# Two layers of convolutional self-attention in float32 on one core: loops written out, and the prologue's statistics, staging and second projection in a new order

## The chip, the cores and the metric

The kernel runs on 1 core of one Trainium2 chip. The metric is the device time in microseconds, median of several runs. Of one more run there is a profile with every instruction of every engine; its span is the time from the first to the last instruction, and times in the trace count from the span's start.

## The reference, cut to what matters

Both layers compute, for each of 8 images of 256 channels and 32 x 32 = 1024 positions:

```python
xn  = group_norm(x, 32 groups) * gamma + beta
qkv = w_qkv @ xn + b_qkv                 # 8 heads of 32 channels
m   = softmax((q / 32**.25).T @ (k / 32**.25))     # 1024 x 1024 for each head
out = x + w_proj @ (m @ v) + b_proj
```

The second layer takes the first one's output, has weights of its own and no bias on q, k and v. Everything is float32.

## The kernel before

There are 16 blocks (layer and image), and each is worked through in two slots of 4 heads, so 32 slots, numbered 0 to 31. In a slot 64 units follow each other (2 halves of 512 queries x 8 tiles of 128 keys x 4 heads). For each unit TensorE multiplies a tile of transposed scores (`scores_t`, L396), ScalarE takes the exponential (`exp`, L631), and TensorE later multiplies it with the values (`weighted_values`, L442). The softmax needs the maximum of each query's row before. So another score tile per unit, in the other orientation, runs 40 units ahead (`AHEAD`): `scores_for_max` (L421) on TensorE, `max_unit` (L708) on VectorE, three PSUM banks in turn, so that TensorE is at most three units ahead of VectorE. After each eight of them VectorE reduces once more (L716), and SP copies that head's row of negative maxima into row 96 of the queries by four small transfers (`load_row`, L300); row 96 of the keys holds ones, so that `scores_t` subtracts the maximum. `scores_t` waits for its row at the first tile of each head and half.

q and k are kept as a float32r part and the rest. `project_qk` (L464) on TensorE makes a half of q or k in four matmul instructions, `qk_high` (L650) on ScalarE writes the high part, `qk_low` (L725) on VectorE the low one, both into staging tiles. From there SP copies for each head three pieces of q and three of k, 32 partitions of 4 KB each (`stage_head`, L290), so that one matmul over 96 partitions has all three products. `project_v` (L472) and `v_out` (L733) make the values. All this is done for the next slot or block in between the units, at fixed places (`DENSE_AT` and others), and so are group statistics: `channel_stats` (L741) and `add_quarters` (L746) on VectorE, `mean_square` and `scale_and_shift` on GpSimd, `group_stats` (L487) on TensorE, `group_stats_out` (L656) and `normalise` (L663) on ScalarE. GpSimd sums the exponentials (L876).

Each engine's program is written by hand and runs in its own order; semaphores tie them together. TensorE's program is written out in full (`write_slots`). ScalarE, VectorE and GpSimd use `run_slots`: slot 0 plain, then a loop of 7 passes over 4 slots (slots 1 to 28), then slots 29 to 31 plain. In the loop the semaphore values to wait for are computed in registers. SP's program has slots 0 to 4 plain, a loop of 2 passes (slots 5 to 12), slots 13 to 16 plain, a loop of 3 passes (slots 17 to 28), and the rest plain.

Before slot 0 there is a prologue. Image 0 is loaded, then weights, then image 1. Image 0's statistics (VectorE, GpSimd, TensorE, ScalarE) lead to its normalising; TensorE projects q and k of the first four heads into four banks, then the values; ScalarE and VectorE empty the banks. SP waits until all low parts are written (`qkl_done` 4) and issues the 24 staging copies. VectorE, behind its value evacuations, does image 1's statistics; TensorE multiplies them (`group_stats(1, ps_v)`), and then 40 leading units of `scores_for_max` follow (w = 0 to 39). Between them TensorE projects q and k of the other four heads: part r after unit w = 8r, its low part on VectorE after unit w = 8r + 2. ScalarE's first `qk_high` of these overwrites the staging tiles, so it waits until all 24 copies are done.

Of the kernel before, what the change touches and what calls it, by code (L numbers as in the profile page):

```python
# [25 lines left out]
F32 = mybir.dt.float32  # L26
# [8 lines left out]
HD = C // HEADS  # L35
SCALE = float(HD) ** -0.5
P = 128
CT = C // P
HG = HEADS // CT
NT = S // P  # L40
HALF = 512
NH = S // HALF
# [21 lines left out]
ROWS_AT = 7  # L64
STATS_AT = (23, 26, 28, 33)
# [17 lines left out]
def plain(n):  # L83
    return Slot(n, n // 2, n % 4)


def looped(i, k):
    return Slot(LOOP_SLOTS * i + LOOP_FROM + k, 2 * i + (LOOP_FROM + k) // 2, (LOOP_FROM + k) % 4)
# [6 lines left out]


def run_slots(eng, slot):

    slot(plain(0), first=True)
    with eng.Fori(0, LOOPS) as i:  # L100
        for k in range(LOOP_SLOTS):
            slot(looped(i, k))
    for n in range(LOOP_FROM + LOOPS * LOOP_SLOTS, SLOTS):
        slot(plain(n), has_next=n + 1 < SLOTS, has_second=n + 2 < SLOTS, has_third=n + 3 < SLOTS)
# [54 lines left out]
def attention_layers(nc, x, w_qkv, w_proj, pars, bias_v, bias_proj, ident_in, group_in, out):  # L159
    nc.disable_value_cache = True  # L160
    ctx = ExitStack()
    with ctx:
# [96 lines left out]
        def _(sp):  # L259
# [57 lines left out]
            sp.dma_start(wp[:, :, :], w_proj[0]).then_inc(wproj_loaded, 16)  # L317
            for h in range(HG):
                stage_head(0, 0, h)
# [46 lines left out]
            with sp.Fori(1, turn) as i:  # L366
                body(i, 0, 0)
            body(turn, 1, 0)
            with sp.Fori(turn + 1, LOOPS) as i:
                body(i, 1, 1)  # L370
# [9 lines left out]
        def _(pe):  # L380
# [103 lines left out]
            def group_stats(j, bank):  # L484

                pe.wait_ge(mv_summed, j + 1)
                mm = pe.matmul(bank[:, 0:2 * CT], group[:, :], channel_mv[:, :, :], start=True, stop=True)  # L487
                mm.then_inc(gm_ready, 1)
# [86 lines left out]
            for r in range(4):  # L575
                for kt in range(CT):
                    project_qk(0, 0, r, kt, start_banks[r])
            for r in range(4):

                pe.wait_ge(qkl_done, r + 1)  # L580
                for t in range(2):
                    project_v(0, r, t, start_banks[r])
            pe.wait_ge(gm_done, 1)
            group_stats(1, ps_v)

            pe.wait_ge(v_done, 4)
            pe.wait_ge(ones_row_set, 2)

            for w in range(AHEAD):
                scores_for_max(-1, 1, w - AHEAD + UNITS)  # L590
                if w % MAX_GROUP == 0 and w // MAX_GROUP < 4:
                    r = w // MAX_GROUP
                    if r:

                        pe.wait_ge(qkl_done, 4 + r)
                    for kt in range(CT):
                        project_qk(1, 0, r, kt)
            write_slots(slot)
# [15 lines left out]
        def _(act):  # L614
# [74 lines left out]
            for part in range(CT * NH):  # L689
                normalise(1, 1, part)  # L690
# [3 lines left out]
            run_slots(act, slot)  # L694
# [4 lines left out]
        def _(dve):  # L699
# [109 lines left out]
            add_quarters(0)  # L809
            for r in range(4):  # L810
                qk_low(0, 0, 0, r, start_banks[r])
# [4 lines left out]
            for part in range(CT * NH):  # L816
                channel_stats(1, 1, part)
            add_quarters(1)
            for w in range(AHEAD):
                max_unit(-1, w - AHEAD + UNITS)  # L820
                if w % MAX_GROUP == 2 and w // MAX_GROUP < 4:
                    qk_low(1, 1, 0, w // MAX_GROUP)
            run_slots(dve, slot)
# [6 lines left out]
        def _(pool):  # L830
# [62 lines left out]
            scale_and_shift(0, 0)  # L893
            for b in range(2):
                pool.memset(ks[b][MROW:MROW + 1, :, :].bitcast(F32), 1.0).then_inc(ones_row_set, 1)

                pool.wait_ge(ones_row_set, b + 1)
            mean_square(1)
            scale_and_shift(1, 1)
            run_slots(pool, slot)  # L900


# [46 lines left out]
```

## Time and profile before

| | us |
|---|---|
| median of 3 runs | 2149.19 (2148.03 to 2149.98) |
| profiled execution | 2149.15 |
| its span | 2147.4 |
| TensorE busy | 2092.4 (97%) |
| GpSimd busy | 1791.0 (83%) |
| VectorE busy | 1696.5 (79%) |
| ScalarE busy | 1238.8 (58%) |

Busy time is the sum of an engine's instructions. A busy share near 100% in a stretch means that the engine sets the pace there; where it is lower, the rows say what the engine waited for. TensorE's clock has two levels; the granted clock is 1.00 where it had the full one and 0.50 where it had half. A row of the windows below has: start and end of the stretch, its length, then busy time (and number of instructions) of TensorE's matmuls, its weight loads, VectorE, ScalarE and GpSimd, then the granted clock, the DMA engines' mean busy share and GB/s. A row of a timeline has: start, length, engine, line, what it writes and reads, how many in a row, and in brackets the idle time before it with what ended it.

### The profile page before, as it was taken

To read this page: it belongs to the slowest core of one execution; us is meant where nothing else is said; L and a number is where in the kernel's file an instruction comes from. 1 tells how busy PE (TensorE), PEld (TensorE's weight loads), DVE (VectorE), ACT (ScalarE), POOL (GpSimd) and SP (SyncE) were. 2 spreads that over 40 slices of the span, in tenths; PEclk is the share of its full clock that TensorE was granted. 3 is DMA by queue.
4 is the path that set the end of the run, shared out by engine and by line. 5 is a ranking of instruction groups with operands and counts; after the bars stand their busy time and mean duration, and the time that the engine had idled before them with its cause. 6 is when DMAs were issued, how large, how long until landed. Compare 5 with 4: busy or idle time off the path is not lost.

```text
span 2147.4 us, 37263 instructions
## 1 busy us (share of the span) xinstructions
PE 2092.4 (97%) x10552; PEld 1160.0 (54%) x10552; DVE 1696.5 (79%) x2896; ACT 1238.8 (58%) x2321; POOL 1791.0 (83%) x567
## 2 busy tenths in 40 slices
PE   5999999999999999999999999999999999999998
PEld 3455555555555555555555555555555555556542
DVE  3878888788887888887887888878887788888881
ACT  2355656566565665656565565655656556565654
POOL 2398988888887988978988888978889889889895
PEclk8799999999999999999999999999999999999999
DMA  4333243322334233244322434223343222433211
GB/s 125 60 57 63 61 100 80 92 44 59 84 80 100 62 68 65 65 100 99 85 50 52 98 79 99 55 56 70 80 99 75 70 56 60 99 80 80 54 27 40
DMA packets 208741, 157.04 MB, mean 73 GB/s; under 512 B 166528, under 2 KB 166784, under 8 KB 208512
## 3 DMA queue, kind: packets, MB, share of 16 engines
q1 hardware_dynamic: 208512, 154.48, 32.0%
q8 instruction: 84, 1.38, 0.3%
q14 instruction: 145, 1.19, 0.2%
HBM read 36.39 MB, written 16.78 MB: 25 GB/s over the span
## 4 chain that ended last, share of the span: by engine, by line
PE 90%; POOL 4%; issue 2%; DVE 2%; SPq 1%; ACT 1%; DMA 1%; DVEq 0%; ACTq 0%; POOLq 0%
PE ps_t L396 23%; PE ps_m L421 21%; PE ps_v L442 21%; PE ps_d L464 10%; PE ps_m L456 6%; PE ps_d L479 5%; PE ps_d L472 5%; POOL acc L876 3%; DVE raw_max L708 1%; SPq L290 1%; ACT pt L631 0%; DMA qs<-neg_max 0%; PE ps_m L464 0%; DMA par<-pars_dram 0%; PE ps_t L487 0%
## 5 line engine op out<-in xcount | busy, mean ns | idle before, releaser
L631 ACT ACTIVATE pt<-ps_t 128x512 f32<-128x512 f32 x2048 | 1110.2, 599 | 835.2 <-PE ps_t L396 823.5
L708 DVE TENSOR_REDUCE raw_max<-ps_m 128x1 f32<-128x512 f32 x2048 | 1316.8, 685 | 304.7 <-PE ps_m L421 265.2
L876 POOL TENSOR_TENSOR acc<-acc,pt 128x2048 f32<-128x2048 f32 x317 | 1450.7, 4576 | 32.7 <-POOL gn_c L861 5.5
L421 PE MATMUL ps_m<-ks,qs 96*128 96x512 f32 x2048 | 994.1, 487 | 14.4 <-DVE raw_max L708 13.2
L396 PE MATMUL ps_t<-qs,ks 97*128 97x512 f32 x2048 | 842.9, 413 | 13.1 <-ACT pt L631 11.7
L396 PEld LDWEIGHTS ps_t<-qs,ks 97*128 97x128 f32 x2048 | 389.7, 190 | 379.3 <-ACT pt L631 158.6
L876 POOL TENSOR_TENSOR acc<-pt 128x2048 f32<-128x2048 f32 x64 | 292.7, 4573 | 264.8 <-ACT pt L631 264.8
L421 PEld LDWEIGHTS ps_m<-ks,qs 96*128 96x128 f32 x2048 | 391.8, 191 | 193.2 <-DVE raw_max L708 115.0
L442 PE MATMUL ps_v<-pt,v 128*32 128x512 f32 x4096 | 492.7, 597 | 0.0
L464 PE MATMUL ps_d<-xn,wq 128*128 128x512 f32 x500 | 263.6, 611 | 5.8 <-ACT xn L663 5.8
L442 PEld LDWEIGHTS ps_v<-pt,v 128*32 128x32 f32 x4096 | 119.5, 109 | 250.4 <-issue 171.0
L479 PE MATMUL ps_d<-att,wp 128*128 128x512 f32 x256 | 130.8, 593 | 3.8 <-DVE att L764 2.9
L472 PE MATMUL ps_d<-wq,xn 128*128 128x256 f32 x488 | 125.1, 378 | 0.0
L464 PEld LDWEIGHTS ps_d<-xn,wq 128*128 128x128 f32 x500 | 98.1, 197 | 31.5 <-issue 11.0
L472 PEld LDWEIGHTS ps_d<-wq,xn 128*128 128x128 f32 x488 | 92.3, 189 | 17.5 <-issue 0.5
L753 DVE STREAM_TRANSPOSE turned<-ps_m 128x512 f32<-128x512 f32 x64 | 45.9, 717 | 40.4 <-PE ps_m L456 38.8
L716 DVE TENSOR_REDUCE neg_max<-raw_max 128x4 fp32r<-128x8 f32 x256 | 41.4, 162 | 41.3 <-DVE raw_max L708 40.2
L456 PE MATMUL ps_m<-pt,ones 128*32 128x512 f32 x536 | 71.6, 607 | 0.3 <-DVE raw_max L708 0.2
L456 PE MATMUL ps_m<-acc,ones 128*32 128x512 f32 x512 | 68.6, 595 | 0.0
L725 DVE SCALAR_TENSOR_TENSOR stage_ql<-ps_d,par,stage_qh 128x512 fp32r<-128x512 f32 x63 | 47.3, 751 | 21.0 <-ACT stage_qh L650 15.0
L479 PEld LDWEIGHTS ps_d<-att,wp 128*128 128x128 f32 x256 | 48.6, 191 | 17.5 <-issue 5.2
L775 DVE SCALAR_TENSOR_TENSOR res<-ps_d,bp,res 128x512 f32<-128x512 f32 x64 | 47.5, 743 | 12.2 <-PE ps_d L479 12.2
(49 smaller groups left out, 540.2 us busy)
## 6 DMA issues: line engine op xcount, KB each, us to landing
ks<-stage_kh SPq DMA_DIRECT2D x256, 128.0 KB, 2.4
qs<-stage_qh SPq DMA_DIRECT2D x256, 128.0 KB, 2.4
ks<-stage_kl SPq DMA_DIRECT2D x128, 128.0 KB, 2.4
qs<-stage_ql SPq DMA_DIRECT2D x128, 128.0 KB, 2.5
qs<-neg_max SPq DMA_DIRECT2D x1024, 0.5 KB, 2.0
xn<-x_dram SPq DMA_DIRECT2D x16, 512.0 KB, 4.5
res<-x_dram SPq DMA_DIRECT2D x16, 512.0 KB, 4.5
between<-res SPq DMA_DIRECT2D x32, 256.0 KB, 2.3
```

The source lines that it names most:

```text
L396: pe.matmul(ps_t[score_bank(s.g, u)][:, :], ks[s.qk][0:KROWS + 1, h, t * P:(t + 1) * P], qs[s.qk][0:KROWS + 1, h, hf * HALF:(hf + 1) * HAL ...
L421: pe.matmul(ps_m[max_bank(u)][:, :], qs[b][0:KROWS, h, c:c + P], ks[b][0:KROWS, h, kf * HALF:(kf + 1) * HALF], start=True, stop=True).then ...
L442: mm = pe.matmul(ps_v[HD * h:HD * (h + 1), :], v[s.v][:, t, c:c + HD], pt[t % 4][:, h, :], start=(t == 0), stop=(t == NT - 1))
L456: mm = pe.matmul(ps_m[bank][HD * h:HD * (h + 1), :], ones[:, :], tile[:, h, :], start=(k == 0), stop=(k == len(tiles) - 1))
L464: mm = pe.matmul(bank[:, :], wq[:, kt, c:c + P], xn[parity][:, kt, hf * HALF:(hf + 1) * HALF], start=(kt == 0), stop=(kt == CT - 1))
L472: mm = pe.matmul(bank[:, t * C:(t + 1) * C], xn[parity][:, kt, (2 * r + t) * P:(2 * r + t + 1) * P], wq[:, kt, 2 * C:3 * C], start=(kt == ...
L479: mm = pe.matmul(ps_d[:, :], wp[:, kt, ct * P:(ct + 1) * P], att[:, kt, hf * HALF:(hf + 1) * HALF], start=(kt == 0), stop=(kt == CT - 1))
L631: act.activation(pt[t % 4][:, h, :], ps_t[score_bank(s.g, u)][:, :], ACT.Exp, scale=SCALE).then_inc(exp_done, 1)
L708: dve.tensor_reduce(raw_max[:, e % 2, t, kf:kf + 1], ps_m[max_bank(u)][:, :], AX.X, ALU.max)\
L725: dve.scalar_tensor_tensor(out=lo[:, cols], in0=bank[:, :], scalar=par[:, parity, 4 + 2 * which + g:5 + 2 * which + g], in1=hi[:, cols].bi ...
L775: dve.scalar_tensor_tensor(out=r, in0=ps_d[:, :], scalar=bp[:, ct:ct + 1], in1=r, op0=ALU.add, op1=ALU.add).then_inc(proj_done, 1)
L876: pool.tensor_tensor(acc[hf][:, :, :], a[:, :, :], pt[t % 4][:, :, :], ALU.add).then_inc(pool_added, 1)
```

## The change

- `run_slots` and the loops of SP's program are gone. All engines use `write_slots`, and SP's `for` runs in Python, so that every slot's instructions stand in the program with constant semaphore values.
- In the prologue VectorE does image 1's statistics right behind image 0's. TensorE's `group_stats(1, ps_v)` stands ahead of the value projection. GpSimd's `mean_square(1)` and `scale_and_shift(1, 1)` stand ahead of the memsets of the ones rows, and TensorE waits for these only ahead of slot 0.
- The 24 staging copies of the prologue are issued by two engines: the 12 into the queries by SP, the 12 into the keys by ScalarE behind `group_stats_out(1, ps_v)`.
- The second projection's part r stands after unit w = 8r + 6 (before: 8r), its low part after unit w = 8r + 10 (before: 8r + 2). ScalarE normalises a quarter of image 1 after each of its four `qk_high` (before: all four ahead of them).

```diff
+START_QK, START_LOW = 6, 2
...
-def run_slots(eng, slot):
-
-    slot(plain(0), first=True)
-    with eng.Fori(0, LOOPS) as i:
-        for k in range(LOOP_SLOTS):
-            slot(looped(i, k))
-    for n in range(LOOP_FROM + LOOPS * LOOP_SLOTS, SLOTS):
-        slot(plain(n), has_next=n + 1 < SLOTS, has_second=n + 2 < SLOTS, has_third=n + 3 < SLOTS)
...
@@ SP @@
-            for h in range(HG):
-                stage_head(0, 0, h)
+            sp.wait_ge(qkl_done, NH)
+            for h in range(HG):
+                for r, part in enumerate(("qh", "qh", "ql")):
+                    sp.dma_start(qs[0][HD * r:HD * (r + 1), h, :].bitcast(F32),
+                                 stage[part][HD * h:HD * (h + 1), :].bitcast(F32)).then_inc(staged[h], 16)
...
-            with sp.Fori(1, turn) as i:
+            for i in range(1, turn):
                 body(i, 0, 0)
             body(turn, 1, 0)
-            with sp.Fori(turn + 1, LOOPS) as i:
+            for i in range(turn + 1, LOOPS):
                 body(i, 1, 1)
@@ TensorE @@
+            pe.wait_ge(gm_done, 1)
+            group_stats(1, ps_v)
             for r in range(4):
 
                 pe.wait_ge(qkl_done, r + 1)
                 for t in range(2):
                     project_v(0, r, t, start_banks[r])
-            pe.wait_ge(gm_done, 1)
-            group_stats(1, ps_v)
 
             pe.wait_ge(v_done, 4)
-            pe.wait_ge(ones_row_set, 2)
-
             for w in range(AHEAD):
                 scores_for_max(-1, 1, w - AHEAD + UNITS)
-                if w % MAX_GROUP == 0 and w // MAX_GROUP < 4:
+                if w % MAX_GROUP == START_QK and w // MAX_GROUP < 4:
...
+
+            pe.wait_ge(ones_row_set, 2)
@@ ScalarE @@
-            for part in range(CT * NH):
-                normalise(1, 1, part)
+
+            act.wait_ge(qkl_done, 4)
+            for h in range(HG):
+                for r, part in enumerate(("kh", "kl", "kh")):
+                    act.dma_start(ks[0][HD * r:HD * (r + 1), h, :].bitcast(F32),
+                                  stage[part][HD * h:HD * (h + 1), :].bitcast(F32)).then_inc(staged[h], 16)
 
             for r in range(4):
                 qk_high(1, 1, 0, r)
-            run_slots(act, slot)
+                normalise(1, 1, r)
+            write_slots(slot)
@@ VectorE @@
             add_quarters(0)
+            for part in range(CT * NH):
+                channel_stats(1, 1, part)
+            add_quarters(1)
...
-            for part in range(CT * NH):
-                channel_stats(1, 1, part)
-            add_quarters(1)
             for w in range(AHEAD):
                 max_unit(-1, w - AHEAD + UNITS)
-                if w % MAX_GROUP == 2 and w // MAX_GROUP < 4:
-                    qk_low(1, 1, 0, w // MAX_GROUP)
-            run_slots(dve, slot)
+                if w % MAX_GROUP == START_LOW and w >= MAX_GROUP:
+                    qk_low(1, 1, 0, w // MAX_GROUP - 1)
+            write_slots(slot)
@@ GpSimd @@
             scale_and_shift(0, 0)
+            mean_square(1)
+            scale_and_shift(1, 1)
             for b in range(2):
                 pool.memset(ks[b][MROW:MROW + 1, :, :].bitcast(F32), 1.0).then_inc(ones_row_set, 1)
 
                 pool.wait_ge(ones_row_set, b + 1)
-            mean_square(1)
-            scale_and_shift(1, 1)
-            run_slots(pool, slot)
+            write_slots(slot)
```

## Rows read from the trace of the kernel before

**Rows 1.** The page: busy time, share of the span, instructions.

```profile
PE 2092.4 (97%) x10552; PEld 1160.0 (54%) x10552; DVE 1696.5 (79%) x2896; ACT 1238.8 (58%) x2321; POOL 1791.0 (83%) x567
```

**Rows 2.** Windows of slots 1, 3, 5, 25, 28 and 29.

```profile
136.53:201.68 65.15, 64.72 (x340) 37.59 (x338) 54.14 (x94) 37.48 (x72) 55.51 (x24) 1.00 0.43 82
...
265.49:330.07 64.58, 64.50 (x340) 37.69 (x338) 54.12 (x94) 37.36 (x72) 54.68 (x23) 1.00 0.36 83
...
393.76:461.22 67.46, 65.02 (x339) 37.67 (x338) 54.02 (x94) 37.35 (x72) 54.62 (x23) 1.00 0.34 80
...
1690.95:1758.15 67.20, 65.03 (x339) 37.67 (x338) 54.02 (x94) 37.36 (x72) 54.58 (x23) 1.00 0.34 80
...
1886.56:1950.25 63.69, 63.69 (x321) 34.51 (x320) 52.03 (x89) 39.93 (x75) 57.67 (x14) 1.00 0.31 68
1950.25:2013.92 63.67, 63.67 (x338) 37.31 (x336) 51.85 (x89) 37.69 (x71) 54.70 (x13) 1.00 0.31 67
```

**Rows 3.** Timeline around slot 5's start: start, length, what, [idle before, releaser].

```profile
396.58 1.57 ACT L631 ACTIVATE pt<-ps_t 128x512 f32<-128x512 f32 x3 [2.26 <-PE ps_t L396]
...
398.32 1.89 DVE L708 TENSOR_REDUCE raw_max<-ps_m 128x1 f32<-128x512 f32 x3 [3.20 <-issue]
...
399.06 0.50 PE L421 MATMUL ps_m<-ks,qs 96*128 96x512 f32 x1 [1.33 <-DVE raw_max L708]
```

**Rows 4.** Table of waits, whole run: total, times, longest.

```profile
DVE raw_max L708 <- issue: 18.2, 6, 3.2
```

**Rows 5.** Timeline of slot 1, and its wait in the whole run's table.

```profile
171.49 0.47 PE L396 MATMUL ps_t<-qs,ks 97*128 97x512 f32 x1 [0.36 <-DMA qs<-neg_max]
...
PE ps_t L396 <- DMA qs<-neg_max: 0.4, 1, 0.4
```

**Rows 6.** The prologue: timeline of SP's first and last staging copy, then windows.

```profile
27.71 0.64 SPq L290 DMA_DIRECT2D ks<-stage_kh  x1
...
42.35 0.60 SPq L290 DMA_DIRECT2D qs<-stage_ql  x1
...
12.00:13.00 1.00, 0.00 (x0) 0.00 (x0) 0.00 (x0) 0.00 (x0) 0.77 (x4) 1.00 0.03 10
...
29.00:44.00 15.00, 10.21 (x31) 6.40 (x30) 6.60 (x11) 3.10 (x5) 2.59 (x11) 0.77 0.91 206
...
45.80:52.60 6.80, 5.25 (x8) 2.41 (x8) 4.50 (x8) 0.11 (x1) 0.00 (x0) 0.50 0.03 0
80.00:90.00 10.00, 9.92 (x43) 5.94 (x42) 8.13 (x16) 6.63 (x13) 4.54 (x1) 0.83 0.41 79
```

**Rows 7.** Timeline of the prologue from the last value evacuation on.

```profile
33.11 0.69 DVE L733 TENSOR_TENSOR v<-ps_m,bv 128x512 f32<-128x512 f32 x1 [1.03 <-PE ps_m L472]
33.72 2.46 DVE L741 BATCH_NORM_STATS2 stats<-xn 128x6 f32<-128x512 f32 x4
37.46 0.56 PE L487 MATMUL ps_v<-channel_mv,group 128*128 128x4 f32 x2 [4.39 <-DVE channel_mv L746]
37.88 0.77 PE L421 MATMUL ps_m<-ks,qs 96*128 96x512 f32 x1
38.69 0.69 DVE L708 TENSOR_REDUCE raw_max<-ps_m 128x1 f32<-128x512 f32 x1 [1.38 <-PE ps_m L421]
45.22 0.69 ACT L650 ACTIVATE stage_qh<-ps_d,par 128x512 fp32r<-128x512 f32 x1 [1.59 <-DMA qs<-stage_ql]
45.94 0.75 DVE L725 SCALAR_TENSOR_TENSOR stage_ql<-ps_d,par,stage_qh 128x512 fp32r<-128x512 f32 x1 [2.12 <-ACT stage_qh L650]
46.61 3.07 DVE L708 TENSOR_REDUCE raw_max<-ps_m 128x1 f32<-128x512 f32 x5
49.20 3.60 PE L464 MATMUL ps_d<-xn,wq 128*128 128x512 f32 x4
53.06 1.29 DVE L708 TENSOR_REDUCE raw_max<-ps_m 128x1 f32<-128x512 f32 x2 [2.58 <-PE ps_m L421]
79.00 0.63 PE L396 MATMUL ps_t<-qs,ks 97*128 97x512 f32 x1
```

## The prediction

> **What bounds the kernel now.** I read the page's busy line first: TensorE is busy 97% of the span, 2092.4 of 2147.4 us, no other engine over 83% [rows 1]. So time can be won only where TensorE stands idle, some 55 us. The windows then place it: I cut the trace at the first transposed-score matmul (L396) of each of the 32 slots. A slot of odd number with statistics takes 64.58, 64.56, 64.57 us (slots 3, 7, 27) and TensorE is busy for all but 0.1 us of it. Slots 5, 9, 13, 17, 21 and 25 take 67.20 to 67.46 us with 2.2 to 2.4 us idle [rows 2]. They are the first slot of a repeated pass of the loops. The zoom on slot 5 says why: ScalarE's first exponential comes 2.26 us late though its matmul is done, VectorE then idles 3.20 us with "issue" as its only cause, and TensorE waits 1.33 us for VectorE alone [rows 3]. The table of waits has this "issue" wait exactly six times, 18.2 us in all [rows 4]. Slot 1, where the loops are entered without a jump back, has none of it, and slot 29, straight code on every engine after the loops, none either [rows 2]. The jump back is what costs.
>
> The rest is at the start: the first L396 runs at 79.00 us [rows 7]. The chain there is: projections; 24 staging transfers issued one by one by SP, 27.71 to 42.95 us, 0.635 us each [rows 6]; ScalarE's first evacuation of the second projection, which waits for the last of them until 45.22; VectorE's low part, 45.94 to 46.69, before which only three of the 40 leading maxima are done; then 37 maxima and three more projections up to slot 0 [rows 7].
>
> **The change, part by part.** *Loops written out.* It removes six jumps back. Six slots sum to 403.75 us (67.46, three of 67.27, 67.28, 67.20); at slot 3's length they are 6 x 64.57 = 387.4, a gain of 16.3. The nearest other row is slot 1: 65.15 us, 0.57 longer than slot 3. It lost this at 171.49, where TensorE waited 0.36 us for SP's row of negative maxima to land [rows 5]. The late jumps covered that: a TensorE that comes 2.7 us later finds its rows there. If all six slots hit it, the gain is 6 x 2.13 = 12.8. The table of waits has such a wait once in the whole run [rows 5], so I charge one hit, 0.6, and take 15.7. The register instructions of the loops go too. Slot 29 without them and without group statistics takes 63.67, even slot 28 with them 63.69 [rows 2]: they are hidden behind TensorE, and I take 0. The end of the range: where a slot's statistics make TensorE wait for ScalarE, 14 times, each may lose about one 0.1 us step, 1.4 us of gain in all.
>
> SP's own straight code issues the same transfers in the same order; only its late arrival behind the jump goes. For the fetching of more code I take 0; the cover is that it runs ahead, as for TensorE's program, and its failing is a rival below.
>
> *Statistics of image 1 earlier.* VectorE's four (2.46 us at 33.72) and the quarter sum move into its idle time before 20.75. Their image is there: the DMA share is down to 0.03 in 12 to 13 us [rows 6]. They end near 15, and nothing waits. TensorE's group matmul moves ahead of the V projection and pushes that back by its 0.42 us (37.46 to the next matmul at 37.88). The last V evacuation, 33.11 to 33.80, ends at 34.2, and the leading scores start at 34.3 instead of 37.88 [rows 7]. Head 0 must be staged by then: its last transfer was issued at 30.92 and two queues don't make it later. GpSimd's memsets of the ones rows (7.07 us) go behind its scaling, to end at about 37, long before their new wait at the first slot. Normalising image 1, 2.93 us of ScalarE, is spread between evacuations; the first slot wants it 22 units in. Both cost 0.
>
> *Staging on two queues.* SP issues the q copies, ScalarE the k copies. Issue alone would shrink from 15.2 us to 12 x 0.635 = 7.6, and the last copy would land at 37.4. But in 29 to 44 us the 16 DMA engines are busy 0.91 already, at 206 GB/s [rows 6]. So 16 us of landing (29 to 45) can shrink to 0.91 x 16 = 14.6: 1.4 us earlier, 43.6. Issue of a DMA by ScalarE isn't in this trace; nearest is SP's 0.60 us, so 7.6 us there, ending at 35.3, or later if the full engines hold it back. Queued behind it is only the evacuation that waits for all 24 copies anyway. Bounds for the term: 0 to 1.4.
> The Trainium skill, "DMA: Bandwidth & Descriptors", section "Issuing engines are not separate DMA queues", says the same against this edit: transfers from several queues run on the same 16 engines, and only issue time is saved. By issue time alone the last landing would be 7.6 us earlier, by the rule with this trace's 0.91 1.4 us.
>
> *Second projection later among the leading scores.* It moves from the 1st, 9th, 17th and 25th unit to the 7th, 15th, 23rd and 31st, the low parts from the 3rd to the 11th and on. So VectorE isn't stopped after three maxima. From 34.3 (first maximum about 0.7 later, as 38.69 follows 37.88) it does 11 maxima at 0.614 us (5 in 3.07 [rows 7]), 6.8, and one stall on a projection, 2.6, and is through at 44.4. ScalarE's high part is ready at 43.6 + 0.2 + 0.7 = 44.5. The low part thus ends at 45.3, 1.4 before 46.69, with eight more maxima and a 0.1 us row maximum behind it, 5.0. What follows is as before, three projections, each of which makes VectorE idle (2.58 us at 53.06, the first of three alike, up to 2.8 [rows 7]). Gain 1.4 + 5.0 = 6.4 us. Bounds: 5.0 if the copies land no sooner; about 8 if the first projection stalls VectorE little and the copies come early. The wait for the ones rows, now ahead of the first slot, is long met. The first slot begins at half clock as before: 0.83 granted in 80 to 90 us [rows 6] is a third of ten at half, some 1.7 us lost. It may be none or twice that.
>
> **Sum.** 15.7 + 6.4 = 22.1 us. The profiled execution took 2149.15 us, span 2147.4 and 1.8 around it, which is the median of the runs (2149.19). 2149.15 - 22.1 = 2127.0 us, span about 2125.3.
>
> **Rivals.** *The projection's clock.* In 45.8 to 52.6 TensorE had 0.50, the 1.2 GHz level, after a stretch with less to do, and its four matmuls took 3.60 us [rows 6, 7]. Three earlier projections at 2.4 GHz would take 1.8, and the three stalls of 2.6 would nearly go: 6 us more, 2121.0. Against it: in all three groups the full level came behind the projection and was gone before the next. 8%.
> *The start gains nothing.* Copies on two queues get in each other's way, or the rows of the leading units come late, and the first slot starts at 79 as before: 2149.15 - 16.3 = 2132.9. Against: the DMA engines are idle from 45 on, and VectorE is visibly stopped. 8%.
> *The stall isn't the jump's.* A jump costs next to nothing, and something else in those six slots makes the engines late; it would stay, and only the start's 6.4 us come: 2142.8. Against it: slots 1 and 29 issue the same work and have no such wait [rows 2, 4]. 4%.
> The Trainium skill, "Advanced Engine Details and Errata", section "Control Flow Timing", would have it so: about 108 ns for a compare-and-branch, 0.65 us for six. The trace disagrees, with 3.20 us on VectorE after one jump.
> *Straight code starves.* If ScalarE or VectorE ran out of instructions at each new block of code as they do at the jump, each would cost TensorE some 2.7 us (67.27 - 64.57). From 8 such stalls the gain is gone; one in each of the 28 slots that were looped gives 76 - 22 = 54 us more, 2203. Against: TensorE runs 2 x 10552 instructions [rows 1] straight, and slots 0 and 29 to 31 are straight on all engines; VectorE's only "issue" waits are the six at the jumps [rows 2, 4]. 4%.
>
> **From cases to numbers.** Forecast 2127.0 with 73%, its own range 2123.5 (22.1 + 0.6 for no late row + 1.4 for the statistics + 1.6 for the start at 8) to 2131.5 (12.8 + 5.0 = 17.8). The clock rival adds the low end, 2120.5, the start rival the high end, 2133; left out are the last two and 3% unnamed. About 0.2% (4.3 us) is what a measurement of this kernel can tell from no change. Faster by more: the first three cases, the fourth (6.4 us) and most of the rest, 0.94. Within: 0.02. Slower: 0.04.
>
> **What would show it.** Slots 5, 9, ... 25 at 64.6 us (65.2 where a row is late) and no six "issue" waits: the loops right. The first L396 at 72 to 74 us; SP and ScalarE both issuing from 27.7; ScalarE's first second-projection evacuation near 43.8, not 37.4; the leading scores from 34.3; three stalls of 2.5 us left. Slots of 63.7 and 64.6 elsewhere unchanged. The forecast is wrong if "issue" waits appear in straight code, if rows land late in most odd slots, or if the copies land well after 45.

## The result, and the profile after

| | before | after |
|---|---|---|
| median, us | 2149.15 (2148.03 to 2149.98, 4 runs) | 2118.19 (2112.97 to 2119.25, 4 runs) |
| profiled execution, us | 2149.15 | 2112.97 |
| its span, us | 2147.4 | 2111.2 |
| mean granted clock in it | 0.990 | 0.996 |
| first slot starts at, us | 79.0 | 63.6 |
| slots 1 to 28, us | 1813.7 | 1791.1 |

The ratio is 0.9851 (95% interval 0.9834 to 0.9868): 31 us faster. Forecast were 22.1, 2127.0 us, with a range down to 2120.5. The direction and most mechanisms were right, the size was not. The profiled execution is the fastest of the four by 5 us; why is told in experiment 1. Two executions further down fell in a slow state and count in no ratio: one of experiment 1 (2956.3 us, clock 0.655) and one of the kernel with one queue (2159.8 us, clock 0.944).

From the page of after: TensorE's busy line, then queues (packets, MB, share). In before the last queue, which fetches instructions, had 145 packets and 1.19 MB; q10 is ScalarE's new queue.

```profile
PE 2073.6 (98%) x10552; PEld 1148.2 (54%) x10552; DVE 1698.3 (80%) x2896; ACT 1248.4 (59%) x2321; POOL 1790.4 (85%) x567
...
q10 hardware_dynamic: 576, 1.57, 0.3%
...
q14 instruction: 72, 0.59, 0.1%
```

Windows of after for slots 1, 3, 5, 28 and 29, then for slots 1 to 28 as one:

```profile
120.80:185.15 64.35, 64.21 (x340) 37.45 (x339) 54.14 (x94) 37.86 (x72) 55.94 (x24) 1.00 0.38 83
248.72:313.06 64.34, 64.20 (x339) 37.45 (x338) 54.12 (x94) 37.85 (x72) 55.33 (x23) 1.00 0.42 83
376.64:440.98 64.34, 64.20 (x340) 37.46 (x338) 54.13 (x94) 37.86 (x72) 55.34 (x23) 1.00 0.36 83
...
1848.28:1911.85 63.57, 63.57 (x321) 34.33 (x320) 52.10 (x89) 40.14 (x75) 56.94 (x14) 1.00 0.31 67
1911.85:1975.52 63.67, 63.67 (x337) 37.32 (x336) 51.87 (x89) 37.73 (x71) 54.91 (x13) 1.00 0.31 67
...
120.80:1911.85 1791.05, 1789.11 (x9213) 1004.96 (x9212) 1487.30 (x2535) 1092.03 (x2031) 1572.72 (x492) 1.00 0.34 76
```

Against [rows 2]: slot 5 lost its late start (67.46 to 64.34), but slot 3, which never had one, is shorter too (64.58 to 64.34), and so is slot 28 (63.69 to 63.57). Slot 29, straight code in both, kept its 63.67 to the hundredth.

The start of after, as a timeline, with ScalarE's issues as ACTq:

```profile
23.13 1.26 SPq L313 DMA_DIRECT2D qs<-stage_qh  x2
...
26.57 0.60 ACTq L688 DMA_DIRECT2D ks<-stage_kh  x1
...
33.48 4.28 DVE L708 TENSOR_REDUCE raw_max<-ps_m 128x1 f32<-128x512 f32 x7 [0.59 <-PE ps_m L416]
...
36.36 1.88 PE L459 MATMUL ps_d<-xn,wq 128*128 128x512 f32 x4
...
38.51 0.69 DVE L708 TENSOR_REDUCE raw_max<-ps_m 128x1 f32<-128x512 f32 x1 [0.75 <-PE ps_m L416]
...
39.65 0.69 ACT L645 ACTIVATE stage_qh<-ps_d,par 128x512 fp32r<-128x512 f32 x1 [13.84 <-DMA ks<-stage_kh]
...
41.10 0.74 DVE L725 SCALAR_TENSOR_TENSOR stage_ql<-ps_d,par,stage_qh 128x512 fp32r<-128x512 f32 x1
...
63.56 0.40 PE L391 MATMUL ps_t<-qs,ks 97*128 97x512 f32 x1
```

Against [rows 6, 7]: SP's first copy goes out at 23.1 instead of 27.7, the last has landed by 39.6 instead of 45.2, eleven maxima are done before the first low part instead of three, and a projection takes 1.88 us instead of 3.60 and stops VectorE for 0.75 to 0.89 us instead of 2.6. The windows say what the DMA engines and the clock did (share 1.02, clock 1.00):

```profile
26.50:38.00 11.50, 10.10 (x39) 6.73 (x37) 7.08 (x12) 0.00 (x0) 8.44 (x7) 1.00 1.02 227
...
45.80:52.60 6.80, 4.72 (x13) 2.26 (x13) 5.87 (x12) 1.47 (x3) 0.00 (x0) 1.00 0.05 3
```

Part of this isn't the edit's. The clock became full at 19.8 us here and at 21.9 in before, in the middle of the first projection, whose instructions are the same in both. Its fourth low part ends at 26.54 us instead of 27.68, so everything behind it starts 1.1 us sooner. Over the kernels with the changed order that follow, this low part ends anywhere from 26.3 to 27.8 us (25.4 where the first projection is given a warm clock), whatever the edit behind it. Comparisons of first slots below have to be read with that in mind.

In the profiles the 36.2 us of span are 15.4 before the first slot, 0.3 in slot 0, 22.7 in slots 1 to 28, less 2.2 after them (a stretch at half clock at 2102 fell on the last projection: 3.46 us for four matmuls, 1.96 before).

### The profile page after: what moved, and what is told of

It reads as the page before. It is cut to its first block, busy times and chain, and to the rows that moved or that the text cites. A ratio compares the mean times of both kernels' runs of the same rounds, so it can differ in the third digit from the quotient of the medians.

```text
span 2111.2 us, 31126 instructions
## 1 busy us (share of the span) xinstructions
PE 2073.6 (98%) x10552; PEld 1148.2 (54%) x10552; DVE 1698.3 (80%) x2896; ACT 1248.4 (59%) x2321; POOL 1790.4 (85%) x567
## 4 chain that ended last, share of the span: by engine, by line
PE 93%; POOL 4%; DVE 1%; ACT 1%; issue 0%; DMA 0%; SPq 0%; ACTq 0%; POOLq 0%; DVEq 0%
PE ps_t L391 24%; PE ps_m L416 21%; PE ps_v L437 21%; PE ps_d L459 10%; PE ps_m L451 6%; PE ps_d L474 5%; PE ps_d L467 5%; POOL acc L876 3%; DVE raw_max L708 1%; ACT pt L626 1%; PE ps_m L467 0%; PE ps_m L459 0%; PE ps_t L482 0%; DMA par<-pars_dram 0%; ACT xn L658 0%
## 5 line engine op out<-in xcount | busy, mean ns | idle before, releaser
L626 ACT ACTIVATE pt<-ps_t 128x512 f32<-128x512 f32 x2048 | 1121.9, 599 | 799.0 <-PE ps_t L391 783.5
L708 DVE TENSOR_REDUCE raw_max<-ps_m 128x1 f32<-128x512 f32 x2048 | 1336.6, 686 | 294.4 <-PE ps_m L416 292.2
L459 PE MATMUL ps_d<-xn,wq 128*128 128x512 f32 x500 | 256.8, 596 | 5.7 <-ACT xn L658 5.7
L451 PE MATMUL ps_m<-pt,ones 128*32 128x512 f32 x536 | 71.6, 609 | 0.2 <-DVE raw_max L708 0.2
L775 DVE SCALAR_TENSOR_TENSOR res<-ps_d,bp,res 128x512 f32<-128x512 f32 x64 | 47.5, 743 | 14.2 <-PE ps_d L474 14.2
L645 ACT ACTIVATE stage_qh<-ps_d,par 128x512 fp32r<-128x512 f32 x63 | 43.0, 683 | 21.5 <-DMA ks<-stage_kh 13.8
```

What stands on the lines that cost most here:

```text
L451: mm = pe.matmul(ps_m[bank][HD * h:HD * (h + 1), :], ones[:, :], tile[:, h, :], start=(k == 0), stop=(k == len(tiles) - 1))
L459: mm = pe.matmul(bank[:, :], wq[:, kt, c:c + P], xn[parity][:, kt, hf * HALF:(hf + 1) * HALF], start=(kt == 0), stop=(kt == CT - 1))
L626: act.activation(pt[t % 4][:, h, :], ps_t[score_bank(s.g, u)][:, :], ACT.Exp, scale=SCALE).then_inc(exp_done, 1)
L708: dve.tensor_reduce(raw_max[:, e % 2, t, kf:kf + 1], ps_m[max_bank(u)][:, :], AX.X, ALU.max)\
L775: dve.scalar_tensor_tensor(out=r, in0=ps_d[:, :], scalar=bp[:, ct:ct + 1], in1=r, op0=ALU.add, op1=ALU.add).then_inc(proj_done, 1)
```

## The experiments

**1. Is the start always like this?** The changed kernel unaltered.

> The changed kernel unaltered, to see whether its start always goes as in the profile. Theory A (clock): the granted clock of the prologue differs from execution to execution. Then spans fall with the granted share: about 2111 us at 0.996, about 2116.5 at 0.992 to 0.993, and if this profile has the lower share its first transposed score starts near 68 to 69 us instead of 63.6, with projections that take 3.4 to 3.6 us instead of 1.9; slots 1 to 28 take 1791 us in both. Theory B: the 5 us lie elsewhere (slots or the end); then a slower profile still starts its first slot near 63.6 and slots 1 to 28 take about 1796.

Measured: ratio 0.9855 (0.9829 to 0.9882). Theory A in kind; the first slot is later than its 68 to 69 us. Spans of the two sets of runs go by the granted share: 2111.2 to 2111.7 us at 0.996, 2112.0 at 0.995, 2116.2 to 2116.6 at 0.993, 2117.2 to 2119.9 at 0.992, 2120.3 at 0.991. This profile has 0.992; its timeline:

```profile
36.23 3.33 PE L459 MATMUL ps_d<-xn,wq 128*128 128x512 f32 x4
...
44.60 3.62 PE L459 MATMUL ps_d<-xn,wq 128*128 128x512 f32 x4
...
48.68 0.69 DVE L708 TENSOR_REDUCE raw_max<-ps_m 128x1 f32<-128x512 f32 x1 [2.94 <-PE ps_m L416]
...
71.28 0.63 PE L391 MATMUL ps_t<-qs,ks 97*128 97x512 f32 x1
```

The program is the same and its times agree within 0.2 us up to 36 us; then the first slot comes at 71.3 instead of 63.6, since the projections run at the half clock, 1.2 GHz. Why the clock fell at 36.5 us in one execution and not in the other is open. Slots 1 to 28 take 1790.6. The kernel before spreads in the same way: in the 15 runs beside this one, spans of 2141.3 us at 0.994 to 2154.5 at 0.986. At 0.993 in both kernels it is 2142.8 against 2116.4: 26.4 us at equal clock share, and the other 4.6 of the 31 are a better share. Since the slots give 22.7 of the 26.4, the start and the end together give 3.7 at equal share and 8.3 in the medians.

**2. The loops alone, and the start alone.** The kernel before with only its loops written out:

```diff
-            run_slots(dve, slot)
+            write_slots(slot)
...
```

ScalarE, GpSimd and SP's two loops likewise.

> The kernel before with its loops written out on all engines, prologue as it was. Theory A: the loops' part is 22.7 us, whatever the start: 2126.5 us, first slot at 79 us, slots 5, 9, ... 25 at 64.34 instead of 67.3, other odd slots 64.34 instead of 64.57, even ones 63.6. Theory of the prediction: 15.7 us, 2133.5, since register instructions are hidden. Rival: the start's better alignment is what shortened the slots; then the slots stay at 64.57 and the gain is about 16.

Measured: 2124.95 us, ratio 0.9886 (0.9859 to 0.9912), first slot at 79.1, slots 1 to 28 in 1791.5 us. All 22.2 us of the slots' gain are there with the old start: the rival (the new start shortens the slots) falls, and so does my 15.7.

The changed prologue with the old loops:

> The changed prologue with the loops of before. Theory A: first slot at 63.6 us where the clock is full, 68 to 69 where not; slots as before, with six late starts of 2.7 us; time 2149.2 - 15 = 2134 or, at the lower clock, 2139. If the loops' registers also slow the start, the first slot is later than in the changed kernel at the same clock.

Measured: 2140.45 us, ratio 0.9953 (0.9934 to 0.9973), slots 1 to 28 in 1814.9. It has runs of 2133.7 and 2134.4 at share 0.997 and of 2142.6 to 2143.6 at 0.992; the profile, at 0.992, has its first slot at 71.3 as experiment 1 has. The full clock gave the 2134 that was expected; at the lower clock it is some 4 us more than the expected 2139, 2.3 to 3.3 of them in the first slot's start. The lower clock is the commoner.

**3. Which engine's loop costs it?** The changed kernel with the loop put back on one engine.

> The changed kernel with the loop on VectorE alone. Theory A: the jump costs each engine its own stall; six slots are late by what VectorE's 3.2 us of idleness costs TensorE (1.5 to 2.7 us each), and VectorE's register instructions are the bulk of the 0.24 us of odd slots (64.5). Rival (the stall is ScalarE's, VectorE's is its echo): the six slots are late by under 0.5 us.

> The changed kernel with the loop on ScalarE alone. Theory A (VectorE's loop carries the loops' whole cost, as it did alone: slots 1 to 28 in 1814.0 us): ScalarE's jump makes its exponential 2.2 us late, three score banks cover part of it: the six slots 0.5 to 1.5 us longer than 64.34, the others unchanged at 64.34 and 63.6, slots 1 to 28 in about 1794 to 1800 us. Rival (each engine's jump costs the same alone): 1812 to 1814 us.

> The changed kernel with the two loops of SP alone (slots 5 to 12 and 17 to 28). Theory A: SP's late start of a pass delays rows and copies by up to 3 us but they have slack: slots 1 to 28 in 1791 to 1793 us. Rival: rows of negative maxima land late in the slots behind a jump, 0.5 to 2 us in each of three to five slots.

Windows: slots 3, 5, and 1 to 28 with VectorE's loop; the same with ScalarE's; slots 1 to 28 with SP's.

```profile
252.65:317.29 64.64, 64.49 (x339) 37.69 (x338) 54.12 (x94) 37.85 (x72) 55.35 (x23) 1.00 0.37 83
380.93:448.38 67.45, 64.76 (x339) 37.68 (x338) 54.02 (x94) 37.87 (x72) 55.34 (x23) 1.00 0.35 80
124.17:1938.13 1813.96, 1796.72 (x9213) 1010.67 (x9212) 1485.30 (x2535) 1092.20 (x2031) 1572.67 (x492) 1.00 0.33 75
```

```profile
253.93:318.20 64.27, 64.21 (x340) 37.45 (x338) 54.09 (x94) 37.35 (x72) 55.23 (x23) 1.00 0.36 83
381.76:447.53 65.77, 64.49 (x339) 37.36 (x338) 54.08 (x94) 37.35 (x72) 55.21 (x23) 1.00 0.36 81
126.09:1923.79 1797.70, 1790.53 (x9213) 1004.43 (x9212) 1486.32 (x2535) 1082.76 (x2031) 1572.28 (x492) 1.00 0.33 76
```

```profile
125.50:1917.21 1791.71, 1789.77 (x9214) 1004.45 (x9213) 1486.42 (x2535) 1092.36 (x2031) 1572.61 (x492) 1.00 0.34 76
```

VectorE's loop alone brings back the whole cost, 22.9 us, both the late slots and the 0.3 us of slot 3. ScalarE's brings 6.7, in the six slots only; SP's 0.7. The costs don't add: 22.9 and 6.7 stand against 22.7 for all loops together, whose jumps fall at the same place. GpSimd's loop alone wasn't tried. The zoom at slot 5, first with VectorE's loop, then with ScalarE's:

```profile
385.39 1.89 DVE L718 TENSOR_REDUCE raw_max<-ps_m 128x1 f32<-128x512 f32 x3 [3.11 <-issue]
386.14 0.50 PE L426 MATMUL ps_m<-ks,qs 96*128 96x512 f32 x1 [2.54 <-DVE raw_max L718]
```

```profile
384.76 1.57 ACT L636 ACTIVATE pt<-ps_t 128x512 f32<-128x512 f32 x3 [2.44 <-PE ps_t L401]
385.41 0.50 PE L401 MATMUL ps_t<-qs,ks 97*128 97x512 f32 x1 [1.22 <-ACT pt L636]
```

ScalarE is 2.2 to 2.4 us late in the six slots, VectorE 2.9 to 3.2, but TensorE waits only 1.0 to 1.2 us for ScalarE, and 2.4 to 2.7 for VectorE.

**4. The parts of the start.** Each undoes one part of the changed kernel. SP's wait (NH is 2, the number of halves):

```diff
-            sp.wait_ge(qkl_done, NH)
+            sp.wait_ge(qkl_done, 4)
```

> The changed kernel, but SP waits for all four low parts (qkl_done 4) before its first staging copy, instead of two: one number. Theory A: copying starts 3.4 us later and the engines are full at about 230 GB/s, so the last copy lands 2.5 to 3.4 us later (41.5 to 42.5), and the second projection's first low part, which waits for it, comes 2 to 2.5 us later: 2 to 2.5 us more than the changed kernel of the same clock. Rival: VectorE's maxima set the start, the copies don't: 0 to 0.5 us more.

Measured: 2125.53 us, four runs within 1 us at share 0.991; first slot at 75.0. Against experiment 1 (71.3, also with half clock in the start) 3.7 us, more than the 2 to 2.5 expected. But the fourth low part ended at 27.55 us here and at 26.40 there, before the edit could matter; without these 1.15 us it is 2.6.

All copies by SP, q behind two low parts and k behind four (ScalarE's twelve moved to SP, behind SP's own):

> The changed kernel, but SP issues all 24 staging copies: the 12 of q after two low parts, then the 12 of k after four. Theory A (engines full): one queue moves 206 GB/s instead of 230, so 24 copies take 15.2 us instead of 14.5 and land at about 39.9 instead of 39.2 at full clock. But head 0 is then complete only after 15 copies (about 9.5 us after the first issue at 23.1, 34.5 instead of about 31), so the leading scores begin 1.5 to 2 us later. In all 1 to 2 us more than the changed kernel at the same clock. Rival (the queues matter as issue time): the last copy lands 5 us later and the start is 5 us longer.

Measured: ratio 0.9866 (0.9835 to 0.9897), runs of 2119.1 (0.994), 2120.0 (0.993) and 2126.7 (0.990). At 0.993 and 0.994 it takes 1 to 2 us more than the changed kernel at 0.993. Its first slot at 74.6 in the profile is 3.3 us later than in experiment 1, and 1.3 of them are there at the fourth low part already. Not conclusive.

The second projection back at units 0, 8, 16, 24 and 2, 10, 18, 26:

> The changed kernel, but the second projection's parts after units 0, 8, 16, 24 and low parts after 2, 10, 18, 26, as before. Theory A: VectorE stops after three maxima until the last copy (39.5), the first low part ends at 41, and 37 maxima follow instead of 29: 8 x 0.614 = 4.9 us more, less the 1.0 us that the low part comes earlier: first slot about 4 us later than in the changed kernel at the same clock. Rival: with the copies landing 5.6 us earlier the place no longer matters: under 1 us.

Measured: ratio 0.9880 (0.9856 to 0.9904), first slot at 71.0 with a mixed clock, 7.4 us later than in the one profile of after and as late as in the other. The clock hides what the place is worth.

Image 1's statistics back behind the values:

> The changed kernel, but image 1's statistics on VectorE and TensorE at their old place, behind the values. ScalarE issues the k copies only behind that group result, so they start 9 to 10 us later (36 to 37 instead of 26.6) and the last lands near 44 to 45; head 0 waits for its k: the leading scores begin near 38 to 39 instead of 32.9. Expected: first slot 5.5 to 6 us later at the same clock. Rival: the statistics are cheap and only their own 3.7 us move: first slot under 4 us later.

Measured: 2126.70 us, ratio 0.9900 (0.9875 to 0.9925), first slot at 80.0, 8.7 later than in experiment 1, of which 0.65 at the fourth low part. Expected were 5.5 to 6: right in kind, too small.

**5. Holding the clock.** A matmul without use behind each leading unit that has no projection. It has the operands of that unit's score tile and writes a bank that is free then, for which TensorE waits once:

```diff
+            pe.wait_ge(gm_done, 2)
...
+                if w % MAX_GROUP != START_QK:
...
+                    pe.matmul(ps_v[:, :], qs[0][0:KROWS, h, c:c + P],
+                              ks[0][0:KROWS, h, kf * HALF:(kf + 1) * HALF], start=True, stop=True)
```

> The changed kernel with a second matmul (its result isn't used) behind each leading unit that has no projection, so that TensorE has more to do while VectorE sets the pace; nothing of the output is left out. Theory A (the start's length varies because TensorE's granted clock falls when it has little to do): the clock stays full through the start in every run, the first slot begins at 63.5 to 65 us always, and all runs lie near 2113 with a granted share of 0.996 to 0.997. Rival (the clock falls for a reason outside the kernel): the same spread, 2113 to 2122, or longer since the extra matmuls at half clock take more than VectorE's pace.

Measured: 2113.02 us (2110.18 to 2113.31, 5 runs), ratio 0.9833 (0.9813 to 0.9854), share 0.998 or 0.999 in all. Theory A: with more for TensorE to do in the leading units the clock stayed full there in every run. The window of the leading units (clock 1.00, TensorE busy 26.95 of 30 us) and the group of first slot scores, 64.5 us at the first:

```profile
34.00:64.00 30.00, 26.95 (x89) 14.93 (x87) 26.14 (x46) 5.55 (x8) 1.86 (x1) 1.00 0.21 37
...
L391 PE MATMUL ps_t<-qs,ks x20: 389/398/499, 64.5 to 77.4; 97*128 97x512 f32 x20
```

And three more (`WARM` is 3) before the first projection:

```diff
+            for k in range(WARM):
+                pe.matmul(ps_m[2][:, :], wq[:, 0, 0:P], wq[:, 0, 0:HALF], start=True, stop=True)
             pe.wait_ge(xn_done, CT * NH)
```

> As the one before, and three more matmuls without use before the first projection, while TensorE waits for the normalised image (from about 11 to 16 us). Theory A: the first projection runs at full clock from its start instead of from 19.8 us (3.7 us at half, so 1.8 us to gain), the staging and all behind it come 1.5 to 1.9 us earlier: first slot near 62, 2111.5 us. Rival: the four parts are paced by ScalarE's and VectorE's evacuation, or the extra matmuls delay the projection: no gain or a loss.

Measured: 2110.21 us (2109.16 to 2114.70, 5 runs), ratio 0.9829 (0.9807 to 0.9851).

```profile
12.36 4.64 PE L571 MATMUL ps_m<-wq 128*128 128x512 f32 x6 [2.02 <-DMA wp<-w_proj_dram]
...
16.84 1.88 PE L460 MATMUL ps_d<-xn,wq 128*128 128x512 f32 x4
...
L392 PE MATMUL ps_t<-qs,ks x23: 390/400/504, 62.9 to 79.6; 97*128 97x512 f32 x23
```

The added matmuls hold the first projection back to 16.8 (16.2 in the kernel above), but it then takes 1.88 us instead of 3.75. This is the fastest version. Against the changed kernel it is 8 us less in the medians and about 5 by the ratios, each to its own runs of before; the intervals of the ratios overlap, but only the slowest of its five runs lies within the changed kernel's nine (2112.97 to 2122.13).

**6. The parts of the start with filled units.** With the filled units as base (first slot at 64.5 us) the start can be taken apart. Here the added matmuls write the first score bank, without the wait of experiment 5. The old prologue first, with its loops written out:

> The old prologue with loops written out, and the extra unused matmul behind each leading unit without a projection, as in the filled variant of the changed kernel (first slot at 64.5 us, clock full through the start). Theory A (clock and order are separate gains): at a full clock the old start takes 79.0 less three projection stalls that shrink from 2.6 to 0.8 us and 1 us at the first projection: first slot at 72 to 73.5 us, so the new order is worth 8 to 9 us at equal clock. Rival (much of the 15.4 us was the clock alone): first slot below 69 us.

> The changed kernel with filled units, SP's first copy behind four low parts instead of two. Theory A: last copy 2.5 to 3.4 us later, of which VectorE's lead (about 0.5 us) hides a part: first slot at 66.5 to 67.5 us instead of 64.5. Rival (VectorE's maxima alone set it): 64.5 to 65.

> The changed kernel with filled units and the staging exactly as before: SP alone, behind four low parts, head by head. Theory A: last copy lands near 44 us (26.5 + 15.2 + 2.5) instead of 39.5, so the first low part ends near 46 and the first slot is at 68.5 to 69.5 us; what the earlier wait and the second queue give together is 4 to 5 us. Rival: 1.4 us, the second queue's alone, since the maxima take over: 66.

> The changed kernel with filled units, all 24 copies on SP, q behind two low parts (first issue near 23.1 us), then k. Theory A (the second queue adds little; the earlier start is what counts): 24 copies at 0.635 us are issued by 38.4 and land by 40.8, 1.2 us later than with two queues; head 0 is complete after 15 copies, about 35 us, so the leading scores start 2 us later; first slot at 66 to 67 us instead of 64.5. Rival (a second queue brings the data in 4 us or more faster): 68.5 or later.

> The changed kernel with filled units and the second projection at its old place. VectorE stops after three maxima until the last copy has landed (39.5). Theory A: eight maxima (4.9 us) more behind the first low part, which ends about 0.5 us earlier: first slot at 68.5 to 69.5 us; while VectorE is stopped TensorE has nothing to do, filled or not, so a stretch at half clock may add 1 to 2 us. Rival: 64.5 to 66.

> The changed kernel with filled units and image 1's statistics at their old place, so that ScalarE's k copies start only behind them, at 36 to 37 us. Theory A: last copy near 44.5 to 45, leading scores from 38 to 39: first slot at 70 to 71.5 us. Rival (what is worth something is only VectorE's own 3.7 us): 68.

Measured, one profile of each:

| filled kernel | first slot at | later by | fourth low part ends at | later by, without its shift | us with staging data in flight |
|---|---|---|---|---|---|
| changed (experiment 5) | 64.5 | | 27.0 | | 14.1 |
| one queue, q behind two low parts | 65.4 | 0.9 | 26.3 | 1.6 | 15.5 |
| staging as before | 69.4 | 4.9 | 26.3 | 5.6 | 15.7 |
| second projection early | 70.6 | 6.1 | 27.5 | 5.6 | 14.2 |
| two queues, both behind four | 71.6 | 7.1 | 27.6 | 6.5 | 15.7 |
| old start | 73.9 | 9.4 | 27.1 | 9.3 | 15.7 |
| statistics late | 76.3 | 11.8 | 27.8 | 11.0 | 21.6 |

(The last column is from the first to the last staging packet in the trace. The one before it is my estimate of the edit's own worth: it takes out what the first projection, which no edit touches, was early or late against the 27.0 of the base.) With the matmuls without use the clock stays full from 20.6 us on in the base and from 19.3 with one queue. In the other five kernels 6.8 to 13.7 us at half clock remain behind the first projection, in the old start from 34.7 to 41.6 and from 48.4 to 51.8 us. The old start comes out at 73.9 (expected 72 to 73.5), so clock and order are gains of their own: 79.1 (experiment 2) to 73.9 by the clock that the fill holds (0.6 of it the first projection's shift), 73.9 to 64.5 by the new order and the half clock that is left in the old one. The second queue is worth 0.9 to 1.6 us (expected 1.5 to 2.5), and only because q runs ahead: where both queues start together, the copies need as long as one queue does. Windows of 29 to 37 us, two queues apart, two together, one queue:

```profile
29.00:37.00 8.00, 7.22 (x31) 5.33 (x30) 5.12 (x9) 0.00 (x0) 6.80 (x2) 1.00 1.03 234
...
29.00:37.00 8.00, 7.15 (x32) 5.42 (x30) 4.48 (x8) 0.00 (x0) 7.25 (x4) 1.00 0.96 198
...
29.00:37.00 8.00, 7.22 (x30) 4.94 (x29) 5.34 (x10) 0.00 (x0) 6.05 (x2) 1.00 0.91 206
```

Over the whole transfer the 3.15 MB went at 222 GB/s with the queues apart, 200 with both together and 201 to 204 with one. That both then read the same head's 32 partitions at the same time is my guess for the 198; it wasn't tried.

Where VectorE has to stop for the copies, or ScalarE's issues wait for the statistics, TensorE has nothing to do for 4.2 to 4.8 us at one point, filled or not, and half clock comes on top of the wait. For two queues behind four low parts: ScalarE's evacuation waits until 45.76, TensorE idles 4.79 us, and the window behind it has the clock at 0.50:

```profile
45.76 0.69 ACT L650 ACTIVATE stage_qh<-ps_d,par 128x512 fp32r<-128x512 f32 x1 [18.86 <-DMA qs<-stage_ql]
...
47.89 0.80 PE L416 MATMUL ps_m<-ks,qs 96*128 96x512 f32 x1 [4.79 <-DVE raw_max L713]
...
45.80:52.60 6.80, 4.71 (x7) 2.46 (x8) 3.18 (x6) 1.82 (x3) 0.00 (x0) 0.50 0.02 2
```

With the first projection's shift taken out, SP's wait for four low parts came out dearer than expected (6.5 against 2 to 3) and so did the late statistics (11.0 against 5.5 to 7); the staging as before, at 5.6, is near its 4 to 5, and the early projection, at 5.6, within its 4 to 5 and the 1 to 2 that were expected on top for half clock. How much of each is the half clock wasn't separated. The rivals that called these parts worthless fall. The late statistics are worse than the old start as a whole, because ScalarE issues the k copies only behind them. From experiment 4, that order in the timeline:

```profile
36.83 0.36 PE L482 MATMUL ps_v<-channel_mv,group 128*128 128x4 f32 x2 [4.38 <-DVE channel_mv L746]
37.23 0.60 ACTq L688 DMA_DIRECT2D ks<-stage_kh  x1
...
41.03 4.14 PE L416 MATMUL ps_m<-ks,qs 96*128 96x512 f32 x7 [3.85 <-DMA ks<-stage_kh]
```

## Why the prediction was right or wrong

- **Jumps back: right.** They were priced at 16.3 us from [rows 2]. The six slots went from 403.75 to 386.1, 17.65; without the 0.24 us that other odd slots lost as well, 16.2. The rival on which the jump is cheap and the one on which straight code starves are both out: no engine but TensorE's weight loads has an "issue" wait over 0.2 us in after. On one point the reading of [rows 3] misled: it names VectorE alone. In that trace TensorE also waits 1.03 us for ScalarE at slot 5, and in experiment 3 either engine's loop makes the slot late, by 1.2 to 1.4 us for ScalarE's alone and by all of it for VectorE's.
- **Register instructions: the step that failed, 5.9 us.** I took 0 since slot 29 without them (63.67) and slot 28 with them (63.69) were equal. They aren't the same work: slot 29 is odd, slot 28 even. Written out, slot 28 takes 63.57, and slot 27 takes 64.34 instead of 64.57. Of the 0.91 between slots 27 and 29 I had put everything down to the group statistics; 0.24 went with VectorE's loop. In slot 3 of before VectorE runs 108 register instructions of 71 ns on average, in after none. By the starts of the units in both traces, TensorE loses 0.05 us at unit 12 and 0.03 at unit 44, both behind a half's sums, and 0.21 at unit 28, where VectorE has maxima, statistics and a value evacuation back to back; at unit 54 it regains 0.08. Just ahead of unit 28 in slot 3, before and then after: the row maximum on VectorE has 0.18 us of idle time in front of it, which is gone in after, and the weight load of the next score tile for the maxima waits 0.45 us for VectorE instead of 0.23:

```profile
291.06 0.16 DVE L716 TENSOR_REDUCE neg_max<-raw_max 128x4 fp32r<-128x8 f32 x1 [0.18 <-DVE raw_max L708]
292.53 0.19 PEld L421 LDWEIGHTS ps_m<-ks,qs 96*128 96x128 f32 x1 [0.45 <-DVE raw_max L708]
```

```profile
274.09 0.16 DVE L716 TENSOR_REDUCE neg_max<-raw_max 128x4 fp32r<-128x8 f32 x1
275.49 0.19 PEld L416 LDWEIGHTS ps_m<-ks,qs 96*128 96x128 f32 x1 [0.23 <-DVE raw_max L708]
```

  So a small cost on an engine that is busy 79% does reach TensorE, where TensorE waits for a bank that VectorE still reads. Sum: six slots 1.4, slot 1 0.2, seven other odd slots 1.6, fourteen even ones 2.6. Shown by experiment 3 is that VectorE's loop costs it; that the register instructions do, and nothing else in looped code, is argued from the trace, since no run has the one without the other.
- **Late row: 1.2 us.** I charged 0.6 for one row that lands late; none did, and slot 1's own 0.57 went too. The changed prologue with the old loops has slot 1 at 64.55, the old prologue without loops at 64.36, so neither alone makes the row late; whether it was chance is open. These two steps make 7.0 us, 22.7 instead of 15.7.
- **SP's first copy: misread.** The text has both queues issuing from 27.7. The new wait is for `qkl_done` NH, and NH is the number of halves, 2: the two low parts of q. In the trace of before the second ends at 24.24 and the fourth at 27.68, so the copies may start 3.4 us earlier. The last landed 5.6 us earlier, not 1.4: 3.4 by this wait, 1.1 by the first projection's clock, and 1.0 since the transfer itself was shorter (17.3 us from first issue to last landing before, 16.3 after). With the filled units, wait and queue together are worth 4.9 us as measured, 5.6 at an equal first projection.
- **Second queue: right in size, not in place.** 1.0 us of transfer and 0.9 to 1.6 of the start, against the 1.4 taken from bounds of 0 to 1.4. But that holds with q's copies ahead. As the text had it, both queues from the fourth low part on, the transfer took 15.7 us like one queue's: no gain. The Trainium skill's page "DMA: Bandwidth & Descriptors", section "Issuing engines are not separate DMA queues", has all queues run on the same 16 engines and only issue time saved. The trace agrees in the main: the DMA share went from 0.91 to 1.02 and the rate only from 206 to 227 GB/s.
- **Place of the second projection: right in mechanism** (eleven maxima before the first low part, as forecast), 5.0 us forecast, 5.6 to 6.1 measured with 6.8 us at half clock in it.
- **Statistics: mis-sized.** Their own cost was nothing, as said. But their place also decides when ScalarE issues its copies, which stand behind the group result in its program, and the text has no price for that: with the statistics late the first slot comes 11.0 to 11.8 us later.
- **Clock: the rival at 8% was no rarity.** It is what the profiled run shows (first slot at 63.6, stalls of 0.75 to 0.89 us). In the commoner runs the forecast's kind holds: first slot at 71.3 where 72.6 would have been the sum's. That closeness is partly luck, since 1.3 us of it lie in the first projection and the copies landed for another reason than forecast. The text counts the full level behind the projection "in all three groups" of before; in the trace it is missing behind the one at 57.5 us (0.50 from 56.1 to 69.7). I had treated the clock as a property of the kernel; it is one of the execution, in both kernels, and the four runs of before (within 2 us) hid that.

The median's distance from the forecast, 8.8 us, is 7.0 from the slots; the other 1.8 lie in the start and the end, 8.3 instead of 6.4, and vary with the clock. At equal clock share they gave 3.7, less than the 6.4.

## What to carry to other kernels

Price a loop's registers from two slots of the same work, one in the loop and one outside it, engine by engine; an engine with 20% of idle time can still pass 0.1 to 0.3 us of each 64 us slot on to the one that sets the pace, and one engine's jump can cost as much as all of them together. Read every constant of a wait down to its number before costing what it releases. Where TensorE is paced by another engine for tens of microseconds, look at the clock share of several runs before comparing anything, and hold it with matmuls of no use: that took 5 to 8 us off here and made the other parts easier to measure. Before two starts are compared, look also at the last point that no edit touches; here it moved by up to 1.5 us from run to run.

## What the hardware showed that I had not expected

Written-out code fetched less, not more: the second instruction queue fell from 145 packets and 1.19 MB to 72 and 0.59 MB (109 packets with VectorE's loop alone, 106 with ScalarE's). A jump back idled VectorE for 2.9 to 3.2 us and made ScalarE 2.2 to 2.4 us late. The same program, with the same times up to 36 us, had its first slot at 63.6 us in one execution and at 71.3 in another, and what differs is the granted clock. And two queues that copy from the same staging tiles at once moved 198 GB/s in 29 to 37 us, no more than one queue's 206, while with one of them 3.4 us ahead they moved 234.
